# One unrolled block for combine, masked attention, closing and gated layer of three batches, with all of combine on the vector engine

## What is computed

```python
x = x + _L0_xattn_ref(_layernorm(x), ctx_1024, ctx_1024, ...)      # causal, relative positions
x = x + _L0_ffn_ref(_layernorm(x), ...)                            # 8 experts, 2 for each token
x = x + _L1_xattn_ref(_layernorm(x), ctx_1024, ctx_1024, mask, ...)# masked
x = x + _L1_ffn_ref(_layernorm(x), ...)                            # gated, quantised
```

## Time and profile before

| | us |
|---|---|
| median of three runs (1203.1 to 1204.17) | 1203.2 |
| the profiled execution | 1203.75 |
| its span, first to last instruction | 1202.0 |
| PE busy in the span, clock granted | 1050.5 (87%), 0.932 of full |
| DVE busy | 659.1 (55%) |
| ACT busy | 636.5 (53%) |
| POOL busy | 200.0 (17%) |
| end of the experts' last matmul to the first weighted sum | 719 to 735.5 |
| combine to the first score of the masked attention | 735.5 to 793.0 |
| masked attention, first Exp to last | 802.1 to 1079.7 |
| last group's values and closing | 1079.7 to 1134 |
| gated layer | 1134 to 1202.0 |

### The profile page before, as it was taken

The page is one execution under the profiler, slowest core; times in us unless marked ns, Lnnn a source line. Parts: engine busy times, 40 slices in busy tenths (PEclk is TensorE's granted clock), DMA queues, the critical chain, the costliest instruction groups (busy, mean ns, idle before and its releaser), DMA issues. The chain is left out here.

```text
span 1202.0 us, 21977 instructions
## 1 busy us (share of the span) xinstructions
PE 1050.5 (87%) x6945; PEld 658.6 (55%) x6979; DVE 659.1 (55%) x1993; ACT 636.5 (53%) x1275; POOL 200.0 (17%) x466
## 2 busy tenths in 40 slices
PE   7999999999978698999999991648999999987487
PEld 5555555655545498999999981213333333325254
DVE  4427888888856611211111104857666666775697
ACT  2447877877633232333333321526777777763697
POOL 0000000000000122222222210012222222330222
PEclk9958999999999898999999995869999999998798
DMA  5087898888749336666666644443111111100001
GB/s 184 1 306 293 321 330 322 316 321 324 290 141 360 136 110 226 223 222 219 225 218 222 220 140 153 152 147 91 47 49 46 47 46 46 47 20 10 0 32 40
DMA packets 75342, 199.55 MB, mean 166 GB/s; under 512 B 7880, under 2 KB 40904, under 8 KB 69256
## 3 DMA queue, kind: packets, MB, share of 16 engines
q1 hardware_dynamic: 71528, 188.45, 46.1%
q0 software_dynamic: 3744, 10.23, 2.2%
HBM read 134.82 MB, written 63.83 MB: 165 GB/s over the span
## 5 line engine op out<-in xcount | busy, mean ns | idle before, releaser
L784 DVE CUSTOM_DVE_ANT_0 unused<-mpsS,mask_bias 128x512 bf16<-128x512 f32 x256 | 172.0, 691 | 83.3 <-PE mpsS L717 82.9
L1526 ACT ACTIVATE hT<-ph,w 128x128 f32<-128x128 f32 x312 | 89.2, 369 | 207.7 <-PE ph L1500 207.7
L811 ACT ACTIVATE mPT<-mpsB 128x512 f32<-128x512 f32 x256 | 152.7, 597 | 81.1 <-PE mpsB L724 67.1
L1500 PE MATMUL ph<-xT,w 128*128 128x128 f32 x1248 | 152.1, 282 | 7.5 <-DMA w<-in_w1p 7.1
L1500 PEld LDWEIGHTS ph<-xT,w 128*128 128x128 f32 x1248 | 147.3, 197 | 10.8 <-issue 10.5
L1545 DVE TENSOR_TENSOR xn<-py,b 128x256 f32<-128x256 f32 x39 | 16.6, 425 | 247.4 <-PE py L1510 247.4
L1510 PE MATMUL py<-w,hT 128*128 x624 | 141.2, 379 | 0.7 <-DVE xn L1545 0.7
L659 ACT ACTIVATE scores<-scores,nm 128x512 f32<-128x512 f32 (+3 forms) x256 | 125.6, 557 | 9.8 <-DVE nm L624 9.8
L1510 PEld LDWEIGHTS py<-w,hT 128*128 128x128 f32 x624 | 115.6, 190 | 15.2 <-issue 1.1
L717 PE MATMUL mpsS<-mqk 96*128 96x512 bf16 x256 | 101.2, 397 | 19.5 <-DMA mqk<-packed 15.7
L611 DVE CUSTOM_DVE_ANT_0 scores<-psS,bias 128x512 f32<-128x512 f32 (+3 forms) x176 | 77.8, 487 | 54.6 <-PE psS L552 38.2
(11 more groups left out here) (267 smaller groups left out, 1621.5 us busy)
## 6 DMA issues: line engine op xcount, KB each, us to landing
w<-in_w1p SPq DMA_DIRECT2D x39, 1028.0 KB, 5.8
rel<-stage SPq DMA_DIRECT2D x44, 640.0 KB, 4.6
bias<-rel SPq DMA_DIRECT2D x44, 640.0 KB, 7.1
x<-rel SPq DMA_DIRECT2D x20, 640.0 KB, 6.8
mqk<-packed SPq DMA_DIRECT2D x64, 192.0 KB
w<-in_w2p SPq DMA_DIRECT2D x8, 1024.0 KB, 12.7
rel<-x SPq DMA_DIRECT2D x10, 640.0 KB, 3.2
rel<-mask_bias SPq DMA_DIRECT2D x10, 640.0 KB, 5.0
```

Source lines behind the costliest of these rows:

```text
L784: nc.vector.tensor_tensor_reduce(out=unused[:, i, :], in0=psS[i % 2][:, :], in1=mask_bias[:, i, :], scale=1.0, scalar=-3.0e38, op0=ALU.add ...
L811: nc.scalar.activation(PT[r][:, j, :], psB[j % 2][:, :], ACT.Exp, scale=1.0 / 4).then_inc(s_exp, 1)
L1500: mm = nc.tensor.matmul(ph[half][:, q * P:(q + 1) * P], w1[i][:, dk * F + f * P:dk * F + (f + 1) * P], xT[i][:, dk, :], start=(dk == 0), s ...
L1526: g = nc.scalar.activation(hT[i][:, f, :], ph[half][:, q * P:(q + 1) * P], ACT.Gelu, bias=w1[i][:, DK * F + f:DK * F + f + 1])
```

## The change

The four stages become two. `masked_layer` is one block, written out step by step without a loop, that runs steps n from -16 to 72. `final_batch` is a second block for the closing and gated layer of batch 3 alone, with double-buffered banks, as in the old `closing` and `ffn`.

In `masked_layer` the steps of the attention are as before (the head of step n is n; scores two steps ahead, loads three). Around them hang, slot by slot:

- combine of batch b in the 16 steps from 16(b-1), that of batch 0 in steps -16 to -1, where no attention runs yet. Weighted sums at 1 and 2 steps past the start (one per slot), statistics at 3, norm at 4, apply at 5, transposes at 6, query products at 7 and 8, pieces at 7 to 9, stores at 9 and 10. All of it but the transposes, products and copies is on DVE: also the apply, which ACT did, and the first bf16 piece, which ACT did. The norm (`RowNorm`) takes no square root: it starts from the bits of the variance and makes three Newton rounds, 4 aggregations and 12 small instructions, all on DVE.
- closing of batches 0 to 2 from steps 23, 39 and 55 (five steps each), with norm on DVE and apply and rounding on POOL.
- the gated layer of batches 0 to 2 from steps 28, 44 and 60 (ten steps each, two steps for a tile). `silu(z)` is taken as `z/2 * (1 + tanh(z/2))`: Tanh on ACT and a further product on DVE (`gated`).
- the rounding of the weights in steps 2 to 18.

All of these products share two banks, `psU` and `psX` (the latter also turns the groups' sums). PE waits on `u_free` or `x_free`, the semaphore of whoever last empties that bank, in its own order. The copy of heads into `aN` is gone, since the divided heads go to `xn` in the right layout.

```diff
-    ln = LayerNorm(c1, "c", calls=B, on_scalar=True)
-    q = PieceProjection(c1, "cq", 0, xnT, a["L1_WqT"], None, 4)
-    combine(nc, sem, sb, x, prob, pair_out, ln, q)
-weights = TernaryWeights(nc, a, ctx, sem, sb, banks, xnT)
-masked_attention(mask_bias, maskT, identb, weights)
-tokens = Tokens(ctx, sb)
-closing(nc, a, sem, sb, banks, x, xn, attn, ident, identb, LayerNorm(ctx, "d", calls=B, transposed=False, on_scalar=True), weights, tokens)
-ffn(nc, sem, sb, banks, x, identb, weights, tokens, out)
+masked_layer(mask_bias, maskT, identb, prob, wq, ws)
+final_batch(identb, wq, ws)
...
+nc.vector.tensor_scalar(self.sd[:, :].bitcast(I32), self.ve[:, :].bitcast(I32), -0.5, self.SEED,
+                        ALU.mult, ALU.add).then_inc(self.s_rs, 1)
+for k in range(self.ROUNDS):
+    dve.wait_ge(self.s_rs, done + 4 + 3 * k)
+    nc.vector.tensor_tensor(self.t1[:, :], self.sd[:, :], self.sd[:, :], ALU.mult).then_inc(self.s_rs, 1)
+    dve.wait_ge(self.s_rs, done + 5 + 3 * k)
+    nc.vector.tensor_tensor(self.t2[:, :], self.t1[:, :], self.half[:, :], ALU.mult).then_inc(self.s_rs, 1)
+    dve.wait_ge(self.s_rs, done + 6 + 3 * k)
+    nc.vector.scalar_tensor_tensor(out=self.sd[:, :], in0=self.t2[:, :], scalar=1.5, in1=self.sd[:, :],
+                                   op0=ALU.add, op1=ALU.mult).then_inc(self.s_rs, 1)
...
+LOAD, SOFT, ROWS = 3, 2, 1
+FIRST, last = -HEADS, NBH + 2 * GROUP
+CLOSE, FFN = 23, 28
+EARLY = B - 1
...
+def combine_at(n):
+    b, at = n // HEADS + 1, n % HEADS
+    return (b, at) if b < B else (None, None)
+def closing_at(n, i):
+    c, at = divmod(NI * (n - CLOSE) + i, NI * HEADS)
+    return (c, at) if 0 <= c < EARLY else (None, None)
...
+    c, at = divmod(NI * (n - FFN) + i, NI * HEADS)
+    if not 0 <= c < EARLY or at >= 5 * ROUND:
+        return None, None, None
+    t, k = divmod(at, ROUND)
+    now = NI * c + t if t < NI else None
+    return now, (NI * c + t - 1 if t > 0 else None), k
...
+            if m % ROUND == 0:
+                sp.wait_ge(s_qout[m % HEADS // ROUND], 3 * 16 * (m // HEADS + 1))
+            wait(sp, s_bmm, NI * (m - RING + 1))
+            load_head(sp, m, qk[slot][0:KP, :], s_qk[slot])
...
+            if b is not None and (at, i) in ((7, 0), (8, 2)):
+                pe.wait_ge(*u_free)
+                queries(b, at - 7)
+                u_free = s_qf, DK * b + at - 7 + 1
+            if c is not None and at in (4, 6):
+                pe.wait_ge(*x_free)
+                projected(c, at // 2 - 2)
+                x_free = s_res, 2 * c + at // 2 - 1
+            if c is not None and at == 18:
+                pe.wait_ge(*u_free)
+                tokens_turned(c)
+                u_free = s_qc, c + 1
+            now, prev, k = ffn_at(n, i)
+            if now is not None and k in (0, 4):
+                pe.wait_ge(*u_free)
+                wide(psU, 0, now, k // 4, s_g)
+                u_free = s_a, 2 * now + k // 4 + 1
+            if now is not None and k in (1, 5):
+                pe.wait_ge(*x_free)
+                wide(psX, 1, now, k // 4, s_u)
+                x_free = s_h, 2 * now + k // 4 + 1
+            if prev is not None and k == 2:
+                pe.wait_ge(*u_free)
+                hidden_turned(prev)
+                u_free = s_he, prev + 1
+            if prev is not None and k == 7:
+                pe.wait_ge(*x_free)
+                down(prev)
+                x_free = s_y, prev + 1
+            if n % GROUP == 2 and i == 3 and (h := group_at(n, 2)):
+                if x_free:
+                    pe.wait_ge(*x_free)
...
+SPLITS = {(7, 1): (0, 0), (7, 2): (0, 1), (7, 3): (0, 2), (8, 0): (0, 3),
+          (8, 3): (1, 0), (9, 0): (1, 1), (9, 1): (1, 2), (9, 2): (1, 3)}
...
+            if k == 0 and prev is not None and prev % NI > 0:
+                finished(prev - 1)
+            c, at = divmod(NI * (n - FFN - 10) + i, NI * HEADS)
+            if 0 <= c < EARLY and at == 0:
+                finished(NI * c + NI - 1)
+            if now is not None and k in (1, 5):
+                gated(now, k // 4)
+            if now is not None and k in (2, 6):
+                hidden(now, k // 4)
+            if now is not None and k == 6:
+                hidden_top(now)
+            if now is not None and k == 7:
+                hidden_scales(now)
+                if at in (1, 2):
+                    j = 2 * (at - 1) + i // TOPK
+                    t, k = b * NI + j, i % TOPK
+                    nc.vector.scalar_tensor_tensor(out=x[:, t, :], in0=got[:, j, k, :], scalar=prob[:, k, t:t + 1],
+                                                   in1=x[:, t, :], op0=ALU.mult, op1=ALU.add).then_inc(s_x, 1)
+                if at == 5:
+                    lnc.apply(dve, nc.vector, b, b * NI + i, i)
+                if (at, i) in SPLITS:
+                    split(dve, nc.vector, b, *SPLITS[at, i])
+            if b is not None and (at, i) == (4, 0):
+                lnc.norm(dve, b)
+            if c is not None and at in (5, 7):
+                residual(c, at // 2 - 2)
+            if c is not None and at in (8, 9):
+                dve.wait_ge(s_res, 2 * c + at - 8 + 1)
+                for j in (2 * (at - 8), 2 * (at - 8) + 1):
+                    lnd.stats(dve, c * NI + j, j)
+            if c is not None and at == 10:
+                lnd.norm(dve, c)
+            if c is not None and at == 13:
+                largest(c)
+            if c is not None and at == 14:
+                token_scales(c)
...
+            if now is not None and k in (0, 4):
+                gate(now, k // 4)
+            if prev is not None and k == 1:
+                hidden_integers(prev)
+            if prev is not None and k == 2:
+                hidden_out(prev)
```

More of the change, by code:

```diff
@@ L333, in stored @@
                     sp.wait_ge(self.s_out[i], 3 * 16 * self.PARTS // 2)
-        def run_heads(eng, first, last, step):
-            for n in range(first, ROUND):
-                step(n, n % ROUND, n // ROUND)
-            rounds = NBH // ROUND - 2
-            with eng.Fori(1, rounds + 1) as it:
-                for r in range(ROUND):
-                    step(it * ROUND + r, r, it)
-            for n in range((rounds + 1) * ROUND, last + 1):
-                step(n, n % ROUND, n // ROUND)
-        def stage_of(n, r, it, ahead):
-            if isinstance(n, int) and not 0 <= n + ahead < NBH:
-                return None
-            return n + ahead, (r + ahead) % RING, it * (ROUND // RING) + (r + ahead) // RING
@@ new lines, in hidden_integers, with hidden_out @@
+                    def hidden_integers(T):
+                        act.wait_ge(s_hr, T + 1)
+                        wait(act, s_ht, T)
+                        nc.scalar.activation(hq[:, :], hid[T % 2], ACT.Identity, bias=minus_magic[:, :]).then_inc(s_hq, 1)
+                    def hidden_out(T):
+                        act.wait_ge(s_ht, T + 1)
+                        wait(act, s_dn, T)
+                        nc.scalar.copy(hqT[:, :], psUb[:, :]).then_inc(s_he, 1)
+                    for n in range(FIRST, last + 1):
+                        if n % GROUP == 0 and (h := group_at(n, 2)):
@@ L988, in build @@
                             mask_bias, maskT)
+            wq = [sb(ctx, f"wq{n}", [P, 2 * F], BF16) for n in range(3)]
+            ws = sb(ctx, "ws", [P, 3])
             with nc.cleanup_on_exit():
[L990 to L995 removed]
```

1131 lines of the change are left out of this document (606 added, 525 removed).

## The result

The changed kernel takes 1255.17 us (median of three runs, 1252.52 to 1256.82; a fourth, 1750.34 us at a granted clock of 0.55, is left out of the comparison) against 1203.35 for the kernel before: ratio 1.0427, 95% interval 1.0403 to 1.045. It is slower, as forecast (1241, range 1195 to 1285), by 52 us where 38 were forecast. The profiled execution took 1252.52, its span 1250.6.

What follows compares the result with a forecast made beforehand. Masked attention, a PE stretch (266 of 277 us busy), would receive work from stretches where PE has time. Start 780 + steps 387 + tail 28.5 + last block 44.5 = 1240 us span, 1241 forecast, range 1195 to 1285, against 1202 span before.

Steps and rivals of the forecast that it cites:

- The start: Before the 64 steps: batch 0's combine chain, last piece due at 759 us, first score 769, first Exp 780, 22 us earlier than before.
- The tail and the last block: Behind the last Exp: 28.5 us with two tiles at 9.3 each, then 44.5 for batch 3's closing and gated layer.
- The 64 steps: Attention with the merged work, first to last Exp: 387 us, from 780 to 1167; the old loop took 277.
- Closing: Work added per closing in the attention: PE 0.86, 3.5 and 0.6 us; DVE about 7.8, of which the norm is 2.8.
- each step's fullest engine: Pricing of the 64 steps: each costs its fullest engine's work, PE with 0.24 us of waiting; 368 us in all.
- Tile steps: Attention steps with half a gated-layer tile: alternate between 5.9 us of DVE or PE and 5.9 to 6.5 of ACT.
- 0.25 a step: Added to 61 of the 64 steps where DVE work is put between softens: 15 us.
- Low clock: First steps of the loop: some 4 us lost again at PE's low clock.
- Signs to look for: In the new trace: first Exp near 780, steps 25 and 41 near 8.6 us, 24 and 40 near 9.3, last Exp near 1167.
- POOL held by two-input operations: Third rival: DVE's two-SBUF-input operations in combine delay POOL's maxima, 0.5 us each, 9 us: 1250; chance 0.14.
- Evening out: Rival: heavy DVE and PE steps offset each other, PE's sum decides, steps under 349 us: 1180, faster; chance 0.15.
- Lockstep: Rival: every slot of the 64 steps costs its fullest engine, 432 us of steps: 1285, slower still; chance 0.10.

## Why the prediction was right, and where it was off

**Direction and mechanism** were right, and the reason given for them: work was moved from stretches in which PE has time into the one where it has least. The experiments with parts left out show it part by part: each of the three costs more in the steps than it saves outside.

**The start** came at 777.4 for 780; the last piece was done at 759.1 for 759, the first score at 768.4 for 769.

```profile
758.43 0.69 DVE L921 TENSOR_TENSOR pieces<-left,pieces 128x512 bf16<-128x512 f32 x1
...
768.40 1.03 PE L748 MATMUL mpsS<-mqk 96*128 96x512 bf16 x2 [12.67 <-DMA mqk<-packed]
```

**The tail and the last block** were forecast at 73 and took 73.6. A tile behind the last head was forecast at 9.3; DVE's product (L1043) of one tile starts 9.09 us after the other's:

```profile
1180.11 0.69 DVE L1043 SCALAR_TENSOR_TENSOR ctxT<-ctxT,mpsU 128x512 f32<-128x512 f32 x1 [1.05 <-ACT ctxT L1169]
...
1189.20 0.69 DVE L1043 SCALAR_TENSOR_TENSOR ctxT<-ctxT,mpsU 128x512 f32<-128x512 f32 x1 [1.06 <-ACT ctxT L1169]
```

The further product itself took 0.69 (0.72 taken).

**The 64 steps** were forecast at 387 (368 + 15 + 4) and took 399.6. The mis-sized terms:

- *Closing*, 30 us by the count, 44.4 measured. "DVE: about 7.8" counted each operation of DVE, and not that one of them waits for POOL. POOL's applies (1.2 us each, in no sum) stand between the norm and the largest. The step "each step's fullest engine" fails where a chain goes through two engines inside one or two slots: the forecast's list of heavy steps has 25 and 41 (8.6) and leaves 26 and 42 out, and the pairs 25 and 26, 41 and 42 took 16.3 and 17.4 us. Taking POOL out of that chain gave 9.5 us back.
- *Tile steps*: 10 us too little. I had DVE as the fullest engine in some of them; leaving its product out changed nothing that one profile can tell. PE's own work there was priced a little low (down product 0.87, measured 0.98 from start to start), and its waits were covered by 0.25 a step only, where 26 us of tile steps have 2.8 us in which PE isn't busy, 0.7 a step.
- Against these 0.25 us a step, 15 in all, was too much for the steps with combine alone: 306.6 measured for 299 by the bare count, where 15 and 4 on top make 318.

These three close the sum: 14.4 and 9.6 too little, 11.4 too much, 12.6 us. That the steps came within 13 us of the forecast is so in part luck, since errors of 24 and 11 us stood against each other. *Low clock*, 4 us in the forecast for the start alone, isn't a fourth term but lies inside these. The trace has 47 us at the low level, some 31 of them behind gaps at five of the six norms, and filling the gaps gave 4 to 8 us. The forecast counted the six norms as 2.8 us of DVE each and took none of them to lower PE's clock.

**Signs to look for**: steps 24 and 40 were 9.2 us between Exps, for 9.3. Step 25 was 4.9, not 8.6. Its softens are for the head two ahead, so I take its DVE work to show in the Exps of the steps behind; step 26 took 11.4.

**The median** came 2.7 us over the profiled execution, where the sum had put it 0.55 below, as before the change. The changed kernel's runs differ with the granted clock (0.924 for 1252.5, 0.917 for 1256.8). That a kernel whose clock falls often spreads wider isn't shown: the kernel before ran from 1198.85 to 1209.98 on another chip.

**Rivals.** *POOL held by two-input operations* does happen, and is worth next to nothing. In a step with sums of combine:

```profile
866.75 0.20 POOL L942 TENSOR_TENSOR mrest<-mneg,mpieces 128x4 f32<-128x4 f32 x1
866.96 0.48 DVE L1102 SCALAR_TENSOR_TENSOR x<-xnT,prob,x 128x256 f32<-128x256 f32 x1
867.02 0.48 POOL L944 TENSOR_TENSOR mpieces<-mrest,mzero 128x4 bf16<-128x4 f32 x1
```

POOL's operation began beside the sum and ended when it ended (867.44, 867.50): 0.48 in place of 0.20. The Trainium skill (GPSIMD Engine Reference, section Specifications) names such an instruction of VectorE as one that contends; the trace agrees. The rival's sign, a small POOL operation of 0.5 us, thus came (the longest took 0.52), but not its price. It sized the effect at 0.5 us in eighteen steps, 9 us. Over the 64 steps the same operations take between 0.201 and 0.218 us on average in the trace's groups, 0.013 more than their median at most:

```profile
L944 POOL TENSOR_TENSOR mpieces<-mrest,mzero 128x4 bf16<-128x4 f32 x63 | 13.7, 218 | 5.0
```

That is under 2 us in all. *Evening out* needs the steps at under 349 us. Even the kernel built to even the work out took 368.8. *Lockstep* (432 us of steps) is 32 us off on the other side.

## What to carry to other kernels

Before work is moved into a busy loop, price it by what the fullest engine there has left in that very step, and compare with what it costs where it stands: here a tile costs 4.9 us in the attention and 3.54 in a stage of its own, and the two that didn't fit cost some 9 each behind it. Count chains as well as sums: an operation that waits for another engine blocks its whole queue, so put two or three slots between the two. Split any lump that is longer than what the slowest neighbour can buffer, and look at the clock of the busiest engine behind each gap.

## What the runs showed of the hardware

In the changed kernel PE's clock fell at gaps of 1.81, 2.23 and 3.01 us in front of a score inside an otherwise busy stretch, and 512-column bf16 products then started 0.40 to 0.43 us apart in place of 0.22. It didn't fall every time: behind the gap of 1.83 us in the kernel with combine alone it stayed high. The Trainium skill (TensorE: Matmul & The Clock Gate, section "Wait — 56ns, not 53.3ns?") gives 426.7 and 215.7 ns for these; the trace agrees. Twelve products whose results nobody reads, run at each of six norms, went with a granted clock of 0.99 for 0.94 in the steps, and with steps 7.8 us shorter in one profile each (4.0 by the medians).

The Trainium skill (Perfetto Trace Analysis, section Optimization Strategy) says that interleaving regimes with different most-contended engines may improve performance. Here a DVE regime (gated layer) and a PE regime (attention) were interleaved and a tile cost some 1.3 us more than where it stood, since PE still needs 3 us a tile and has 0.24 us a step free; three closings, in which no engine is full, cost 7.1 us each in the steps once their work was spread over slots, and saved 27.7 us behind the last Exp (124.4 us in the version with combine alone, 96.7 with the closings): 6 us of gain.
